# Router logits folded into the node products of a GNN + mixture-of-experts kernel

## The reference, cut to what matters

```
x1  = x + concat(LN(x), agg) @ W.T + b          # agg[dst] = LN(x)[src], the last edge of a node wins; 0 without an edge
tok = LN(x1)
logits = tok @ router_w.T                       # 12500 x 8
p = softmax(logits); top 2, weights normalised to sum 1
out = x1 + tok + sum over the 2 experts of weight * (gelu(tok @ w1[e] + b1[e]) @ w2[e] + b2[e])
```

## Time and profile before

| | us |
|---|---|
| median of 3 timed runs | 1001.22 |
| span of the profiled execution | 1180.7 |
| edge steps | 28.6 to 275 |
| node steps | 275 to 452.6 |
| neighbour stage, until the last `route` | 452.6 to 639.4 |
| sort stage | 639.4 to 692 |
| expert stage | 692 to 1175 |
| busy: PE, DVE, ACT, POOL | 836.3, 868.3, 630.4, 484.9 |

### The profile page before, as it was taken

How to read it: one execution, slowest core, us unless ns; L and a number is a source line. 1 busy time by engine, 2 the same in 40 slices (tenths; PEclk the granted TensorE clock), 3 DMA queues, 4 the chain that set the end, 5 groups by cost and what they waited for, 6 DMA issues and landing times.

```text
span 1180.7 us, 28647 instructions
## 1 busy us (share of the span) xinstructions
PE 836.3 (71%) x9319; PEld 702.9 (60%) x9319; DVE 868.3 (74%) x1893; ACT 630.4 (53%) x1669; POOL 484.9 (41%) x527
## 2 busy tenths in 40 slices
PE   1599888887666862243444468888888888888886
PEld 1588887776555651132333256776766666767766
DVE  6999999995677764477688946776667666766666
ACT  3466666663444331264553345666666565666665
POOL 7000000004445556764650035555555555555554
PEclk9799999999888795555555789999999999999999
DMA  8800000003664444553551712222222222222220
GB/s 228 266 28 27 27 27 27 27 27 84 208 202 149 118 121 144 156 165 99 160 170 63 7 42 68 64 65 61 65 66 64 64 65 66 63 67 65 70 60 11
DMA packets 79211, 104.89 MB, mean 89 GB/s; under 512 B 22593, under 2 KB 64538, under 8 KB 78994
## 3 DMA queue, kind: packets, MB, share of 16 engines
q0 software_dynamic: 21408, 54.87, 16.6%
q1 hardware_dynamic: 57714, 48.76, 14.8%
HBM read 63.16 MB, written 44.01 MB: 91 GB/s over the span
## 4 chain that ended last, share of the span: by engine, by line
PE 31%; DVE 28%; issue 14%; another core or an unknown queue 12%; ACT 8%; DMA 3%; POOL 1%; ACTq 1%; DVEq 1%; SPq 1%; POOLq 0%
PE bank L983 12%; PE bank L997 9%; DVE arena L1099 7%; PE bank L786 6%; DVE arena L1082 5%; ACT arena L750 2%; PE bank L951 2%; PE bank L809 1%; ACT arena L711 1%; DVE bst L1300 1%; DVE arena L1283 1%; DVE big L1297 1%; POOL arena L517 1%; ACT arena L695 1%
## 5 line engine op out<-in xcount | busy, mean ns | idle before, releaser
L983 PE MATMUL bank<-arena,w1s 128*128 128x128 f16 x3000 | 211.2, 220 | 78.0 <-issue 69.1
L983 PEld LDWEIGHTS bank<-arena,w1s 128*128 x3000 | 177.8, 98 | 112.8 <-issue 109.8
L505 POOL DMA_INDIRECT arena<-key_rows,cid x98 | 94.8, 968 | 330.0 <-DVEq L1215 252.7
L750 ACT ACTIVATE arena<-bank,b1s 128x128 f32<-128x128 f32 x500 | 142.0, 368 | 155.6 <-remote 152.1
L532 POOL DMA_INDIRECT out<-arena,gidx x125 | 140.3, 1123 | 188.9 <-DVE arena L1438 149.5
L997 PE MATMUL bank<-w2s,arena 128*128 x1500 | 184.1, 272 | 1.4 <-DVE arena L1418 0.7
L521 POOL DMA_INDIRECT arena<-tok_rows,gidx x125 | 124.4, 995 | 107.4 <-DVE gidx L1407 69.4
L809 PE MATMUL bank<-wgs,arena 128*128 128x256 f16 x1176 | 160.0, 289 | 5.6 <-issue 5.4
L1433 DVE SCALAR_TENSOR_TENSOR arena<-bank,arena 128x256 f32<-128x256 f32 x125 | 60.1, 481 | 132.7 <-remote 129.5
L997 PEld LDWEIGHTS bank<-w2s,arena 128*128 128x128 f16 x1500 | 140.7, 98 | 17.8 <-issue 1.7
L809 PEld LDWEIGHTS bank<-wgs,arena 128*128 128x128 f16 x1176 | 121.7, 104 | 34.1 <-issue 8.6
(11 more groups left out here) (215 smaller groups left out, 1414.9 us busy)
## 6 DMA issues: line engine op xcount, KB each, us to landing
agg_rows<-arena SPq DMA_DIRECT2D x49, 256.0 KB
tok_rows<-arena SPq DMA_DIRECT2D x13, 896.0 KB
big<-x SPq DMA_DIRECT2D x5, 1792.0 KB, 14.1
arena<-w SPq DMA_DIRECT2D x16, 256.0 KB, 2.9
big<-x SPq DMA_DIRECT2D x6, 512.0 KB
arena<-tok_rows,gidx POOLq DMA_INDIRECT x125
out<-arena,gidx POOLq DMA_INDIRECT x125
arena<-key_rows,cid POOLq DMA_INDIRECT x98
```

The lines of the kernel that those rows point to most:

```text
L505: gp.indirect_dma_start(er[:, b % 2, s, :], None, key_rows, bass.IndirectOffsetOnAxis(cid[:, t:t + 1], 0)).then_inc(er_full[b % 2], 16)
L750: last = sc.activation(h32[:, u % 2, at:at + P], bank[2 + u % 2][:, at:at + P], ACT.Gelu, bias=b1s[:, ds(e[x], 1), f], scale=1.0 / SCALE)
L983: last = mm(bank[2 + u % 2][:, at:at + P], parts[x, w, c, f], a[:, u % 4, c * P:(c + 1) * P], start=(n == 0), stop=(n == 5))
```

## The change

The router logits are linear in `x1` up to the normalisation: `tok @ R = (x1 @ R - mean * sum(R)) / std`. And `x1 @ R = x @ R + LN(x) @ (W_self.T R) + (b @ R) + (neighbour part @ R)`. The changed kernel computes these terms for each pair beside the products:

- At the start TensorE composes `W.T R` for both halves, the column sums of R and `b @ R` (`compose`, ahead of its first edge step). SP loads `W` a second time (512 KB) and `b` in columns for it. ScalarE and VectorE split the composed columns in high and low parts (`wxs`).
- `node_linear` writes both halves of a tile into one bank by 6 products of 512 columns instead of 12 of 256. It has the identity product for all pairs, so `add_self` is gone and `take_self` runs for all. Six more products of 24 columns go into `extra`, in the first 48 columns of bank 0 or 1, where `node_transposes` also writes.
- `take_products` has three copies instead of one. The rows of `agg_rows` have 264 floats instead of 256 (the last 8 are the neighbour's share of the logits).
- In the neighbour stage TensorE, `copy_transposed` and `low_turned` have nothing left to do. VectorE computes `us` once for all tiles (`row_logits`), adds the 8 gathered columns per piece, and `route` has two more operations. `route` now stands behind pieces 4, 8, 12 (before 5, 9, 12).

```
 def take_self(i, k):                      # ScalarE; now in every step, after take_products
-    sc.activation(xs[:, ds(2 * i, 2), :]..., bank[2 + k][:, :], ACT.Copy, scale=1.0 / SCALE)
+    sc.activation(xs[:, ds(2 * i, 2), :], linear[k][:, :, 0:D], ACT.Copy, scale=1.0 / SCALE)
 def take_products(i, k, first):           # ScalarE
-    sc.activation(pb[:, k, :], bank[5 + k][:, :], ACT.Copy, scale=1.0 / SCALE).then_inc(agg_copied, 1)
+    sc.activation(pb[:, k, :, 0:D], linear[k][:, :, D:2 * D], ACT.Copy, scale=1.0 / SCALE)
+    sc.activation(pb[:, k, :, D:AROW], extra[:, k, :, 2 * E:3 * E], ACT.Copy, scale=1.0 / SCALE)
+    sc.activation(lx[:, ds(2 * i, 2), :], extra[:, k, :, 0:2 * E], ACT.Copy, scale=1.0 / SCALE
+                  ).then_inc(agg_copied, 1)
...
+compose()                                 # TensorE, ahead of pe_pair(0, 0)
+    pe.wait_ge(s_small, 64); pe.wait_ge(s_wn, 16); pe.wait_ge(row_padded, 2)
+    (12 f32 products of 8 columns into bank 7, then composed + 1)
...
 def node_linear(i, k, first):             # TensorE
     pe.wait_ge(xl_ready, i + 1)
     if not first:
+        pe.wait_ge(self_taken, i - 1)
         pe.wait_ge(agg_copied, i - 1)
     for h in range(2):
-        mm(bank[5 + k][:, h * D:(h + 1) * D], onesh, brow, start=True, stop=False)
-        if early: mm(bank[2 + k]..., idents, xs[:, ds(2 * i + h, 1), :]...)
-        12 x mm(to[:, h * D:(h + 1) * D], a[...], wgs[:, w, c, half * D:(half + 1) * D])
+        to = linear[k][:, h, :]
+        mm(to[:, 0:D], idents[:, :], xs[:, ds(2 * i + h, 1), :]..., start=True, stop=False)
+        mm(to[:, D:2 * D], onesh, brow, start=False, stop=False)
+        6 x mm(to, a[...], wgs[:, w, c, :])
+        6 x mm(extra[:, k, h, :], a[...], wxs[:, w, c, :])
     last.then_inc(g_ready, 1)
 def node_transposes(i, k, first):
     pe.wait_ge(xn_ready, 2 * i + 2)
     if not first:
         pe.wait_ge(xl_ready, i - 1)
+        pe.wait_ge(agg_copied, i - 1)
...
-    for n in range(...): turn(...), logit(...)          # all of TensorE's neighbour stage
...
 def linear_weights():                     # VectorE, edge step 0
-    dve.wait_ge(s_small, 48)
+    dve.wait_ge(s_small, 64)
...
+    dve.wait_ge(wx_high, 1)               # ScalarE: 5 small copies after `composed`
+    ve.tensor_tensor(wxs[:, 1, :, :], wxf[:, :, :], wxs[:, 0, :, :], ALU.subtract)
...
+def row_logits():                         # VectorE, 98 x 8 columns
+    dve.wait_ge(agg_copied, T // 2)
+    (reciprocal, then 5 operations of 784 columns into `us`)
...
 for n, (first, more) in enumerate(PIECES):
     dve.wait_ge(pg_full[n % 2], gathered(n))
+    ve.tensor_tensor(us[:, of, :], us[:, of, :], pg[:, n % 2, 0:more, D:AROW], ALU.add)
     ve.tensor_tensor(xs[:, of, :], xs[:, of, :], pg[:, n % 2, 0:more, 0:D], ALU.add)
...
-    if n >= 1: low_turned(turned(first) - 1)
```

More of the change, by code:

```diff
@@ L185, in gnn_moe @@
         xl = one.take([P, 2, 2 * D], f16)
-        pb = one.take([P, 2, 2 * D], f32)
+        pb = one.take([P, 2, 2, AROW], f32)
         wst = one.take([P, 2, 2 * D], f32)
@@ L204, in gnn_moe @@
         wabs = two.take([P, B], f32)
[L206 to L210, removed]
+        pg = two.take([P, 2, B, AROW], f32)
+        two.at = (34688 + 31) // 32 * 32 if two.at < 34688 else two.at
         b2t = two.take([P, E, D], f32)
+        us = two.take([P, T, E], f32)
+        assert two.at <= 60000
         three = Arena(big, T * D * 4)
@@ L252, in gnn_moe, with psum @@
         ob = four.take([P, DEPTH, D], f32)
-        bank = [ctx.enter_context(nc.psum_tensor(f"bank{i}", [P, 512], f32)) for i in range(8)]
+        def psum(name, banks):
+            return ctx.enter_context(nc.psum_tensor(name, [P, banks * 512], f32))
+        bank01, lin0, bank4, lin1, bank7 = psum("bank01", 2), psum("lin0", 2), psum("bank4", 1), psum("lin1", 2), psum("bank7", 1)
+        linear = [lin0[:, :].rearrange("p (h d) -> p h d", h=2), lin1[:, :].rearrange("p (h d) -> p h d", h=2)]
+        bank = [b[:, n * 512:(n + 1) * 512] for b, banks in ((bank01, 2), (lin0, 2), (bank4, 1), (lin1, 2), (bank7, 1))
+                for n in range(banks)]
+        extra = bank01[:, :].rearrange("p (k n) -> p k n", k=2)[:, :, 0:2 * XC].rearrange("p k (h n) -> p k h n", h=2)
         s_src, s_small, s_wg = sem("s_src"), sem("s_small"), sem("s_wg")
@@ L644, in act_pair @@
                     take_products(i, k, known and i < 2)
[L645 removed]
+                if not known or i >= 0:
                     take_self(i, k)
@@ L776, in _, with compose @@
             pe.wait_ge(consts_ready, 7)
+            def compose():
+                pe.wait_ge(s_small, 64)
+                pe.wait_ge(s_wn, 16)
+                pe.wait_ge(row_padded, 2)
+                for q in range(4):
+                    for o in range(2):
+                        mm(bank[7][:, q * E:(q + 1) * E], wnf[:, o, q * P:(q + 1) * P], rws[:, o, :],
+                           start=(o == 0), stop=(o == 1))
+                for o in range(2):
+                    mm(bank[7][:, 4 * E:5 * E], one32[:, :].broadcast_to([P, P]), rws[:, o, :], start=(o == 0), stop=(o == 1))
+                for o in range(2):
+                    last = mm(bank[7][:, 5 * E:6 * E], bcols[:, o:o + 1].broadcast_to([P, P]), rws[:, o, :],
+                              start=(o == 0), stop=(o == 1))
+                last.then_inc(composed, 1)
             def groups_of_chunks(d):
@@ L807, in node_linear @@
                         for a, w in ((xh, 0), (xh, 1), (xl, 0)):
[L808 to L811, removed]
+                            mm(to, a[:, k, h * D + c * P:h * D + (c + 1) * P], wgs[:, w, c, :], start=False, stop=(n == 5))
+                            n += 1
+                    n = 0
+                    for c in range(2):
+                        for a, w in ((xh, 0), (xh, 1), (xl, 0)):
+                            last = mm(extra[:, k, h, :], a[:, k, h * D + c * P:h * D + (c + 1) * P], wxs[:, w, c, :],
+                                      start=(n == 0), stop=(n == 5))
                             n += 1
@@ L858, in _ @@
             pe.wait_ge(consts3_ready, 10)
[L860 to L902, removed]
             blocks = [(n, min(n + BLK, PAIRS)) for n in range(0, PAIRS, BLK)]
```

147 lines of the change are left out of this document (66 added, 81 removed).

## The result

The changed kernel takes 1021.23 us (median of 4 runs, 1020.18 to 1022.83), the kernel before 1000.3 (4 runs): a ratio of 1.0214, interval 1.0183 to 1.0245. It is slower by 21 us; the forecast was 1030 (993 to 1048). Its profiled execution spans 1018.1 us, though, not the 1139 that a fall of 42 from 1180.7 would give.

A forecast was written before the change was run, and what follows sets the result against it. Bounds taken: VectorE in edge steps, VectorE then GpSimd in node steps, GpSimd's gathers in the neighbour stage, TensorE in experts. +2.5 + 0 + 35 - 5.5 = +32 on 1001.2 gives 1033, less 2.3 of remaining halts: forecast 1030, range 993 to 1048.

The forecast's parts named there:

- a fall of 42 from 1180.7: Whole profiled execution: span changes by 0 to 42 us, down, as TensorE free of neighbour-stage work can't halt there.
- The step that decides: Node steps: transposes wait for ScalarE's copies, closing each pair into a binding round of 6.4 us; +35 us.
- The 23rd step: Node steps: last of the 23 rounds of 6.4 us counted from the low part of pair 25.
- 410 for a kernel without halts: Node steps, kernel before: last pair multiplied at about 407 us and stored 3 us later, against 452.6 in the trace.
- Start: Kernel start: ScalarE waits for another small load, VectorE for `wx_high` and an extra operation; +2.5 us, bounds 0.5 and 8.
- Edge steps: Edge steps: TensorE's added 0.5 us a step is covered by its 1.07 us wait for VectorE; 0.
- Neighbour stage: Neighbour stage: GpSimd's gathers still bind, only the tail gets shorter; -5.5 us, bounds -2 and -12.
- Where the 179.5 us lay: Span over timed median: laid to TensorE halts in the profiled execution, 106 experts, 42 node steps, 42 neighbour stage.
- price everything at the halt-free pace: All stages: timed runs taken as nearly free of halts, so each part of the change is priced without them.
- rival 1: Node steps: round hidden by halts in timed runs, 0 to 10 us from neighbour stage; not slower, say 994; 21%.
- Rival 2: Node steps: pauses drop TensorE to half clock; +31 us if a quarter runs so (1061), 1155 if all; 11%.
- Rival 3: Node steps: pace before nearer 5.8 us a pair, round of 6.0, so +5 there; 1003 us; 8%.

The follow-up runs named there:

- own_banks_3: The changed kernel with the node steps' 24-column sums in banks of their own, transposes no longer waiting, in the 1000 condition: 1008.2 us, ratio 1.0072 to the kernel before.
- before_3: The kernel before, unchanged, run again for its profile in the 1000 condition: 1000.49 us timed, span 998.7.
- before_2: The kernel before, unchanged, run again for its profile in the 1190 condition: 1182.48 us timed.
- the first four kernels: Kernel before again, 1201.17 us; it with only the new wait, 1200.75; changed kernel with separate banks, 1177.32; changed kernel with small copies first, 1180.93.
- the last two: High weights and weight loads moved earlier: in the changed kernel with separate banks, 998.09 us, ratio 0.9979; in the kernel before, 998.14, ratio 0.9982.

## Why the prediction was right, and where not

**The step that decides: right.** The round is there, made of the parts named, and TensorE waits for the small copies 24 times; taking it away (`own_banks_3`) gives 12.3 us at the first gather. But the +35 was laid to the round whole, and the round's wait is less than half of the 26.1 us measured: another 10.5 went with the new order of the weights, and the last 3.3 stayed, where TensorE's own 5.0 us a pair are over the 4.9 and, after the weights, 4.4 us a pair of `before_3`. The terms of the round against the trace above:

| | predicted | measured |
|---|---|---|
| transposes | 0.96 | 0.96 (307.80 to 308.76) |
| products of a tile, the small ones included | 2.10 | 2.00 (308.76 to 310.76), the second tile 2.08 |
| in them, six products of 24 columns | 0.25 | 0.16 (310.60 to 310.76), 27 ns each |
| last issue to the copies | 0.3 | 0.17 (312.68 + 0.16 to 313.01) |
| copies | 0.93 | 0.76 (306.89 to 307.65) |
| back to the transposes | 0.05 | 0.15 (307.65 to 307.80) |
| round | 6.4 | 6.12 |

No single term is far off: the small products take 27 ns where I took 42, near the 46 of 100 columns, and the copies run more into each other than I let them. From pair 25 on there are 22 rounds, 0.28 us shorter each: 6.2 us. The 23rd step was mis-sized: the last pair has no transposes behind it, its products need not wait for the copies, and it follows after 4.15 us and not 6.4 (2.3 us). The first copy is 0.5 us sooner (294.65 for 290.7 + 4.2 + 0.3). Together 8.9 us between a last copy at 442.4 and at 433.5:

```profile
429.32 0.60 ACT L622 ACTIVATE arena<-lin 128x512 f32<-128x512 f32 x1 [3.45 <-PE bank L833]
...
433.47 0.60 ACT L622 ACTIVATE arena<-lin 128x512 f32<-128x512 f32 x1 [2.89 <-PE bank L833]
```

Copies and store took 3.2 us for 3.3. So +26.1 and not +35. The point of comparison, 410 for a kernel without halts, was measured at 410.6, but partly by luck: I had the last pair's store set it. In `before_3` the last copy starts at 405.04, so that store would be in at about 408 (an estimate, with the same 3.2 us), and GpSimd's own search gathers set the 410.6.

**Start: 0, not +2.5.** ScalarE begins at 18.73 instead of 19.57, when its last small load (`bcols`) has landed, and VectorE's low weights start at 26.95 instead of 27.39. The new wait was met:

```profile
26.83 0.21 DVE L1020 TENSOR_TENSOR wxs<-wxf,wxs 128x48 f16<-128x48 f32 x1 [0.19 <-ACT wxs L697]
26.95 1.22 DVE L1023 SCALAR_TENSOR_TENSOR wgs<-arena,wgs 128x1024 f16<-128x1024 f32 x1
```

**Edge steps: 0, as predicted**, with 11.1 us more of TensorE's work in them (222.80 against 211.70).

**Neighbour stage: -6.9 for -5.5, but the stage itself was misread.** I put it at 145 us for a kernel without halts; it takes 161. Of the missing 16 us, 15 are in GpSimd's gathers: one in each piece is not 0.95 us but 1.8 to 2.5. From the changed kernel, VectorE's addition of a piece and the gathers beside it:

```profile
488.26 0.94 POOL L531 DMA_INDIRECT arena<-agg_rows,gat  x1 [0.30 <-issue]
488.69 2.02 DVE L1271 TENSOR_TENSOR big<-big,arena 128x1792 f32<-128x1792 f32 x1
...
489.51 2.02 POOL L531 DMA_INDIRECT arena<-agg_rows,gat  x1 [0.30 <-issue]
491.84 0.95 POOL L531 DMA_INDIRECT arena<-agg_rows,gat  x1 [0.31 <-issue]
```

Both kernels have 13 such long gathers, and each starts while such an addition, of two f32 operands in SBUF, is running; it ends 0.82 us after the addition does (0.81 to 0.84 in all 26). The gather that is already running when the addition begins keeps its 0.95, and so, within 0.1 us, does every gather that starts beside VectorE's statistics, or beside its low parts, which read one operand from PSUM. The changed kernel has three more long ones (1.50, 1.72 and 1.72 us, the stage's first), and they start in operations of `row_logits` and end 0.82 us after them. The 13 of `before_3` take 14.9 us more than 13 of 0.95. That the addition holds the gather is read from these times; no run takes the addition away. The Trainium skill, in "SBUF — State Buffer", section "SBUF: two separate sides", says that VectorE and GpSimd share one pair of ports under an exclusive lock, held for a whole instruction, and that an operation of VectorE with two SBUF inputs takes it too, though only against a GpSimd operation that reads SBUF. The trace agrees with a lock held to the end of the instruction; what of a gather's issue reads SBUF, no run here shows.

The gain against `before_3` is made up so. The three gathers beside `row_logits` make the gathers end 2.0 us later (98 of them in 138.3 us for 136.3), where I had put `row_logits` under a wait. VectorE reaches the addition of piece 13 only 5.8 us after the start of the last gather, and not 10.4, mostly because the low parts of piece 12 no longer stand before the third `route`: -4.6, where I had 1 to 2. And from that addition to the last `route` it is 13.96 us in `before_3` (557.32 to 571.28) and 8.96 now (580.85 to 589.81), with 0.7 for the two more operations in it. Together +2.0 - 4.6 - 5.0 + 0.7 = -6.9: near the -5.5, by terms that were partly off in both directions.

**Where the 179.5 us lay: wrong.** I laid them to the profiled execution, and wrote that timed runs are nearly free of halts. They belong to the condition that the chip is in, in timed runs as well. The spans agree with the timed runs beside them every time (998.7 and 1000.49; 1199.4 and 1201.17). The arithmetic on the halts closed (190 counted, 182.0 between 1180.7 and 998.7), but partly by luck: 42 in the node steps against 42 measured, 106 against 113.9 in the experts, 42 against 25.9 in the neighbour stage. So "price everything at the halt-free pace" was right for the condition in which the 1001.22 was timed, for a wrong reason: the first profile and the first timed runs were not of the same condition. The expected fall of the span failed where it was profiled (1018.1 against a span of 998.7 in that condition). In the other it went from 1180.8 to 1177.1. There rival 1's sign came true: not slower, ratio 0.9898, though by half of its mechanism only. Rival 1 had the round hidden and 0 to 10 us from the neighbour stage; the node steps cost 31 us more there, and the neighbour stage gives back 35, in one profiled execution of each.

**Rival 2**, TensorE at half clock in the node steps, is out: its clock there is 1.00, and 0.95 before, with a pause of 0.94 us in every pair. **Rival 3** is out too: it had pairs of nearly 5.8 us before the change and a round of 6.0; while weights are split, `before_3` has two pairs in 9.8 us, and the round is 6.12.

Sum in the 1000 condition: +2.5 + 35 - 5.5 = 32 predicted; 0 + 26.1 - 6.9 + 0.2 = 19.4 in the span and 21 in the timed runs.

## What to carry to other kernels

When a small result is put into the corner of a buffer that another step reuses, look for the loop that this closes: here 48 columns in the transposes' bank turned a chain with slack into a round that waits on both sides, at 12.3 us for a stage of 24 pairs. Moving work to an engine that looks idle (ScalarE: 53% busy in the first profile) also moves everything queued behind it; doing first what another engine waits for gave 10.5 us in the same stage. And before the 179.5 us between a span and a timed run are explained, have both from the same chip at the same time.

## What the runs showed of the hardware

- The same kernel takes 1000 or 1190 us, timed and profiled alike. In the longer runs TensorE halts between products that, by the profile, wait for nothing. Here are the expert stage's first products from the costliest groups of `before_2` (span 1180.8 us) and then of `before_3` (998.7): busy us, mean ns, then the idle time before them and its releaser.

```profile
L983 PE MATMUL bank<-arena,w1s 128*128 128x128 f16 x3000 | 211.5, 220 | 77.3 <-issue 68.3
```

```profile
L983 PE MATMUL bank<-arena,w1s 128*128 128x128 f16 x3000 | 189.1, 220 | 5.3 <-issue 4.4
```

  The single product takes 220 ns on both and the granted clock is 0.99 on both; the profile puts the idle time down to the issue. The edge steps, where most of TensorE's code is a loop, end at the same time in both (ScalarE's copy of pair 22 starts at 276.06 and 275.50), and the stages that halt are unrolled code; that the code is the reason was not tested. The cause stays open. The chip with the number 6 stands in the records of the first four kernels (1190.92 us) and of the last two (999.64).
- Six products of 24 columns, each with its own weight load, take 27 ns each (310.60 to 310.76).
- A gather's issue of 0.95 us that starts during a VectorE operation with two f32 operands in SBUF ends 0.82 us after that operation, in 29 cases of two traces.
- ScalarE's copy of 32 columns starts 0.06 us after the one of 16 before it (307.39, 307.45), though that one takes 0.18 us.
